# A gated graph step on one Trainium2 core: kept sums added by VectorE instead of merged by TensorE, one early tile more, and pass 2's tiles a step sooner

## The chip, the cores and the metric

The kernel runs on one core of a Trainium2 chip. The metric is the device time of one execution in microseconds (us); lower is better. Before the change it was 345.53 us, the median of 3 runs (345.31 to 345.88). The trace comes from one further, profiled execution.

## What is computed

With 4096 nodes of 64 features and one adjacency matrix `adj` (4096 x 4096, f32, mostly zeros), layer 0 is two gated steps and a layer norm, and layer 1 a sum over each node's last 100 neighbours with weights that halve from one to the next:

```python
def _ggc(x, adj, W, wih, whh, bih, bhh):
    m = adj @ (x @ W)
    gi, gh = m @ wih.T + bih, x @ whh.T + bhh
    r, z = sigmoid(i_r + h_r), sigmoid(i_z + h_z)
    n = tanh(i_n + r * h_n)
    return (1.0 - z) * n + z * x
h = relu(_ggc(x, adj, ...W1)); h = relu(_ggc(h, adj, ...W2))
x = layernorm(x + h)
support = x @ weight
rank = cumsum(adj != 0, axis=1); deg = rank[:, -1:]
k = minimum(deg, 100); pos = rank - (deg - k)
w = (adj != 0) * where(pos > 0, 0.5 ** (k - pos), 0.0)
x = layernorm(x + w @ support + bias)
```

## The kernel before, in words

**Tiling.** The 4096 nodes are 8 chunks of 512 (`NCH`). The matrix comes from memory in pairs of row tiles, 512 KB each: 16 pairs (`NP`) for each chunk. Pairs go into a ring of seven slots (`stream`, `SLOTS`), and a load waits until the pair seven places before it was used by TensorE and read by its mask. SyncE issues the loads in the order of `LOADS`.

**Pass 1** goes through the chunks b = 0 to 7. TensorE multiplies each pair with the first step's input (`product1`, L514) and, where the second step's input for it exists already (`TRI`), also with that. Those partial sums of the second product are set aside for chunks 0 to 4 (`KEPT`): ScalarE copies one half from PSUM into `kept` (chunk 0: `m_high`) at L754, and VectorE adds the other half (`keep_add`, L1109). Between its pairs TensorE runs the recurrence of the chunk before: `gates` (L569), `node` (L598) and a count of the neighbours. VectorE makes a 0/1 mask of each pair (`mask`, L1049); for the pairs in `BY_SIGN` ScalarE does it with a Sign and a Square (`sign_mask`, L757). VectorE also adds up masks and begins the codes.

**Codes and tiles.** The running neighbour count passes from row tile to row tile. `chain` (L1085) is one tile: a subtraction of the mask from the running count (L1096), and the code made of both (L1101). 32 tiles follow each other. The first `N_EARLY` (15) are done in three parts of the columns (`PARTS`: chunks 0 to 2, 3 to 5, 6 and 7), the first two parts in pass 1 at the steps of `CHAIN_EARLY`, the third in pass 2; the others are done whole. After the tile (3, 0) the count is clamped from below over all columns (L1106, "the maximum"). `CHAIN` says which tiles VectorE does in which stage of pass 2, and `CHAIN_CUT` how many of them stand ahead of the sum of squares (L1207), how many between it and `make_x1s` (L1209, the instruction "x1s" L1214), and the rest stands behind.

**Pass 2** has the steps g = 8 to 15 of the recurrence (the second gated step, chunks in descending order). In stage t (t = 1 to 8, g = 7 + t):

- TensorE (`chunk2`, L716): gates(g), two shares of layer 1 (`share`, L618), four pairs of the next chunk, node(g), two shares, the remaining pairs. From stage 7 on there are no pairs, only shares with gates and nodes between them. A chunk whose partial sum was kept gets it back on TensorE: in `product2`, after its first pair, two matmuls of the kept sum with an identity add it in PSUM (L556).
- ScalarE (L907 to 919): two sigmoids (L779), tanh (L786), `high` (the upper half of chunk g+1's product copied to `m_high`, L745), `state` (L802), then expansions (`expand`, L833: a block's codes into bf16 weights for the share, instruction L842), square (L822) of the new nodes, expansions, `split_high` (L826, instruction L832) once x1s is there, expansions. The three numbers in `ACT_EXPANDS[t]` are the expansions in these three places.
- VectorE (L1264 to 1285): first step of the gate's n (L1128), the new state (to L1144), the residual (L1150), `combine` (L1119, the sum of the lower half and `m_high`), tiles, sum of squares, tiles, x1s, tiles, each with expansions by `DVE_EXPANDS[t]` (L1241).
- GpSimd: reciprocal roots (L968), the low half of the support (L982), the bias added (L977).

A share waits for its expansion and for the low half of its support. Each expansion has a place to write to (`PLACE`: weight buffers, dead parts of the codes, `kept` as "k", a dead part of `hx` as "h"). `BY_DVE` and `BY_ACT` say who expands which block, in what order. After stage 8 come the last shares, the last sums and the output (`ACT_END`, `DVE_END`).

Of the kernel before, what the change touches and what calls it, by code (L numbers as in the profile page):

```python
# [50 lines left out]
KEPT = range(0, 5)  # L51
M2_BANK = {0: 3, 1: 1, 2: 2, 3: 3, 4: 2, 5: 3, 6: 1, 7: 2}
# [44 lines left out]
    for first, then in ((1, 2), (1, 2), (2, 4), (3, 5), (3, 5), (4, 6), (5, 8), (6, 9))]  # L97
# [6 lines left out]
CHAIN_EARLY = ({3: (11, 13, 15), 4: (4, 7, 10, 13), 5: (3, 5, 7, 9, 11, 13, 15), 6: (4,)},  # L104
               {6: (10, 11, 12, 13, 14, 14), 7: (2, 3, 5, 6, 7, 8, 9, 10, 12)})
N_EARLY = sum(len(steps) for steps in CHAIN_EARLY[0].values())

BY_SIGN = {5: (8, 11, 13), 6: (8, 9, 11, 13, 14), 7: (1, 8, 9, 11, 13, 14)}
# [42 lines left out]
     if block not in BY_DVE] + \  # L151
    [(4, 3), REST[0], REST[1]] + \
    [block for block in REST[2:] if block not in BY_DVE]
ACT_EXPANDS = {1: (0, 2, 1), 2: (1, 2, 2), 3: (1, 3, 2), 4: (1, 2, 2), 5: (1, 2, 2),
               6: (1, 2, 2), 7: (0, 1, 1), 8: (0, 2, 4)}
DVE_EXPANDS = {1: (0, 0, 0), 2: (0, 0, 0), 3: (0, 0, 0), 4: (0, 0, 1), 5: (0, 0, 1), 6: (0, 0, 3),
# [18 lines left out]
PLACE_USED.update({"m": len(LOADS), "x": NCH * NP, "k": USED[2 * NCH - 3] + 2})  # L175
# [46 lines left out]
CHAIN = [chain_tiles(*x) for x in ((0, 6), (6, 12), (12, 16), (16, 21), (21, 25), (25, 29), (29, 32),  # L222
# [4 lines left out]
def build(nc, adj_t, x_pairs, w1, consts, consts2, bias, out):  # L227
    with ExitStack() as ctx:
# [261 lines left out]
        def _(pe):  # L490
# [46 lines left out]
            def product2(s, q):  # L537
# [202 lines left out]
        def _(act):  # L740
# [93 lines left out]
            def expand(j, i):  # L834
# [72 lines left out]
            for t in range(1, NCH + 1):  # L907
# [90 lines left out]
        def _(dve):  # L998
# [265 lines left out]
            for t in range(1, NCH + 1):  # L1264
# [4 lines left out]
                if t < NCH:  # L1269
                    combine(g + 1)  # L1270
# [107 lines left out]
```

## Time and profile before

| | us |
|---|---|
| median of the runs shown (3) | 345.53 |
| the profiled execution, its own time | 346.18 |
| span of its trace, first to last instruction | 344.1 |
| TensorE busy (matmul) | 328.7 |
| VectorE busy | 299.2 |
| ScalarE busy | 187.6 |
| GpSimd busy | 47.2 |
| moved by DMA | 107.85 MB, of it 106.37 MB read |

The profile is one execution. Its own time is 2.1 us above the span, for what lies before the first and after the last instruction. Busy matmul time is modelled and overlaps at its ends, so a row that starts before the row ahead of it has ended is no error. TensorE's granted clock is at full rate (2.4 GHz) for all of the work. Times in the rows count from the start of the span. Pass 1 ends at about 192 us, pass 2's pairs at about 294 us.

### The profile page before, as it was taken

What the parts mean: (1) busy time and instruction counts of PE and PEld (TensorE: products, weight loads), DVE (VectorE), ACT (ScalarE), POOL (GpSimd) and SP (SyncE); (2) the same over time, 40 slices, a digit from 0 to 9 for tenths busy, and PEclk for the clock granted to TensorE, in tenths of its full rate; (3) what the DMA queues carried; (4) which work ended last, traced back from release to release, by engine and by line L of the source; (5) the groups of instructions that cost most, each with busy time, mean ns of one, the idle gap of its engine ahead of it and who ended that gap; (6) DMA issues with size and microseconds to landing.
All of it is one profiled execution on the core that took longest, in us unless ns stands there. A gap on an engine that the chain in (4) does not pass through costs nothing.

```text
span 344.1 us, 6780 instructions
## 1 busy us (share of the span) xinstructions
PE 328.7 (96%) x2540; PEld 154.0 (45%) x2540; DVE 299.2 (87%) x494; ACT 187.6 (55%) x245; POOL 47.2 (14%) x50
## 2 busy tenths in 40 slices
PE   1998999999999999999999999999999999999993
PEld 0442334333333333333333333546364544789993
DVE  0689879899999999997999678878999999968996
ACT  0203304105122047068467437897977869768995
POOL 2000000000000000000000001250514232233275
PEclk9999999999999999999999999999999999999999
DMA  6999999999999998999898999998999996000003
GB/s 240 414 410 409 410 407 410 404 402 367 399 396 370 366 392 327 351 360 352 291 336 301 378 368 381 392 344 324 339 379 391 346 381 249 4 16 4 2 2 123
DMA packets 32143, 107.85 MB, mean 313 GB/s; under 512 B 3568, under 2 KB 6512, under 8 KB 32112
## 3 DMA queue, kind: packets, MB, share of 16 engines
q1 hardware_dynamic: 31248, 106.15, 81.4%
q10 hardware_dynamic: 864, 1.28, 1.1%
q8 instruction: 20, 0.33, 0.4%
q14 instruction: 11, 0.09, 0.1%
HBM read 106.37 MB, written 1.05 MB: 312 GB/s over the span
## 4 chain that ended last, share of the span: by engine, by line
PE 78%; DMA 10%; DVE 8%; issue 2%; POOL 0%; ACT 0%; POOLq 0%; ACTq 0%; DVEq 0%; SPq 0%
PE m_acc L509 41%; PE out L509 17%; DMA stream<-in_adj_t 9%; PE out L647 8%; PE gate_ps L585 4%; DVE codes L1241 3%; PE gate_ps L592 3%; PE m_acc L647 2%; DMA w<-in_w 2%; PE gate_ps L609 1%; PE gate_ps L614 1%; DVE s_in L1298 1%; DVE codes L1052 1%; DVE stream L1305 1%; PE m_acc L556 1%
## 5 line engine op out<-in xcount | busy, mean ns | idle before, releaser
L509 PE MATMUL m_acc<-stream,s_in 128*64 128x512 f32 x488 | 119.1, 596 | 1.2 <-DMA stream<-in_adj_t 0.9
L1052 DVE TENSOR_SCALAR codes<-stream 128x1024 uint8<-128x1024 f32 x109 | 71.8, 686 | 6.4 <-DMA stream<-in_adj_t 6.2
L509 PE MATMUL out<-stream,s_mid 128*64 128x512 f32 x264 | 66.3, 593 | 0.0
L968 POOL TENSOR_TENSOR rstd<-stat,mhalf 128x4 f32<-128x4 f32 (+1 forms) x17 | 25.6, 1510 | 277.2 <-DVE stat L1207 277.1
L509 PEld LDWEIGHTS m_acc<-stream,s_in 128*64 128x64 f32 x488 | 32.8, 136 | 63.7 <-issue 48.4
L509 PE MATMUL m_acc<-stream,s_mid 128*64 128x512 f32 x224 | 51.8, 600 | 0.2 <-DMA stream<-in_adj_t 0.2
L1101 DVE SCALAR_TENSOR_TENSOR codes<-codes,run 128x384 uint32<-128x384 uint32 (+2 forms) x62 | 45.4, 732 | 2.1
L1096 DVE TENSOR_TENSOR run<-run,codes 128x768 uint16<-128x768 uint16 (+2 forms) x61 | 43.6, 715 | 2.0
L745 ACT ACTIVATE m_high<-m_acc 64x512 f32<-64x512 f32 x13 | 7.7, 594 | 56.3 <-PE m_acc L509 47.7
L842 ACT ACTIVATE wexp<-codes,code_bias 128x2048 uint16<-128x2048 uint8 x18 | 35.7, 1992 | 0.1
L509 PEld LDWEIGHTS out<-stream,s_mid 128*64 128x64 f32 x264 | 18.9, 137 | 37.1 <-issue 36.4
L779 ACT ACTIVATE rz<-gate_ps,b_rz 128x256 f32<-128x256 f32 x32 | 13.4, 468 | 37.7 <-PE gate_ps L592 37.6
L509 PEld LDWEIGHTS m_acc<-stream,s_mid 128*64 128x64 f32 x224 | 14.6, 136 | 26.4 <-issue 25.3
L842 ACT ACTIVATE codes<-codes,code_bias 128x2048 uint16<-128x2048 uint8 x12 | 23.6, 1990 | 0.0
L1069 DVE TENSOR_TENSOR wexp<-wexp,codes 128x2048 uint16<-128x2048 uint16 x16 | 19.6, 1225 | 2.5 <-issue 2.0
L1241 DVE TENSOR_SCALAR codes<-codes 128x2048 uint16<-128x2048 uint8 x15 | 18.7, 1285 | 0.0
L786 ACT ACTIVATE n_g<-t_n,const 128x256 f32<-128x256 f32 x16 | 8.1, 508 | 15.0 <-DVE t_n L1132 14.8
L764 ACT ACTIVATE codes<-codes 128x1024 uint8<-128x1024 int8 x14 | 14.8, 1057 | 0.4
L761 ACT ACTIVATE codes<-stream 128x1024 int8<-128x1024 f32 x13 | 13.6, 1044 | 0.2 <-DMA stream<-in_adj_t 0.2
L802 ACT ACTIVATE mx<-hx 64x256 f32<-64x256 f32 x32 | 13.2, 414 | 0.8
L1128 DVE SCALAR_TENSOR_TENSOR t_n<-gate_ps,const,rz 128x256 f32<-128x256 f32 x16 | 7.7, 479 | 6.6 <-ACT rz L779 6.6
L1002 DVE COPY s_in<-gate_ps 128x256 f32<-128x256 f32 x8 | 3.4, 419 | 11.1 <-PE gate_ps L500 11.1
(179 smaller groups left out, 413.4 us busy)
## 6 DMA issues: line engine op xcount, KB each, us to landing
stream<-in_adj_t SPq DMA_DIRECT2D x192, 512.0 KB, 6.1
wexp<-in_adj_t SPq DMA_DIRECT2D x2, 512.0 KB, 5.5
late<-in_adj_t SPq DMA_DIRECT2D x2, 512.0 KB, 6.6
third<-in_x_pairs SPq DMA_DIRECT2D x8, 128.0 KB, 6.2
out_nodes<-stream SPq DMA_DIRECT2D x7, 128.0 KB, 2.0
hx<-in_x_pairs ACTq DMA_DIRECT2D x1, 512.0 KB, 7.1
third<-in_adj_t SPq DMA_DIRECT2D x1, 512.0 KB, 8.0
run<-in_adj_t SPq DMA_DIRECT2D x1, 512.0 KB, 9.5
```

Of the source, the lines that this page charges most:

```text
L509: last = nc.tensor.matmul(to[D * u:D * (u + 1), :], state[:, t * D:(t + 1) * D], data[:, u * CW:(u + 1) * CW], start=start[u], stop=stop)
L585: nc.tensor.matmul(to[e * D:(e + 1) * D, 0:HW], w_rz[layer][:, part * D:(part + 1) * D], mx[:, e * HW:(e + 1) * HW], start=True, stop=True)
L647: last = nc.tensor.matmul(end_bank(i, t)[:, t * P:(t + 1) * P], w[:, k * CW + t * P:k * CW + (t + 1) * P], half[:, k, :, :], start=first a ...
L761: nc.scalar.activation(to.bitcast(I8), loaded(n), ACT.Sign)\
L764: nc.scalar.activation(to, to.bitcast(I8), ACT.Square).then_inc(squares_made, 1)
L842: nc.scalar.activation(weights(j, i).bitcast(U16), block(j, i), ACT.Relu, bias=code_bias[:, :], scale=float(P)).then_inc(by_act, 1)
L968: nc.gpsimd.tensor_tensor(rstd[:, r, nodes], stat[:, r, nodes], mhalf[:, nodes], ALU.pow).then_inc(rstd_made, 1)
L1052: nc.vector.tensor_scalar(edges(p // 2, b, 2 * (p % 2), 2), loaded(n), 0.0, None, ALU.not_equal).then_inc(mask_made, 1)
L1069: nc.vector.tensor_tensor(to, left, right, ALU.add).then_inc(sum_made, 1)
L1096: nc.vector.tensor_tensor(running(n + 1, U16)[:, to], running(n, U16)[:, to], tile_edges(c, k, U16)[:, to], ALU.subtract)\
L1101: nc.vector.scalar_tensor_tensor(at, at, EDGE_BIT, running(n, U32)[:, to], ALU.logical_shift_left, ALU.bitwise_or)\
L1241: nc.vector.tensor_scalar(weights(j, i).bitcast(U16), block(j, i), float(P), -float(P * CODE_ZERO), ALU.mult, ALU.add)\
```

## The change

- TensorE no longer merges the kept sums (the matmuls at L556 go). For the steps 11 to 15 (`WITH_KEPT`) VectorE makes `m_high` by one addition of the upper half in PSUM and the kept sum (`high_kept`), between residual and combine of the stage before the step, and ScalarE's `high` goes for those steps.
- 16 tiles instead of 15 are begun in pass 1. In chunk 4 there are six early tiles instead of four, in chunk 6 none of part 0 (before: one, at step 4) and seven of part 1 (before: six).
- Chunk 4 gets three ScalarE masks, at its steps 8, 11 and 13.
- Stage 2 of pass 2 does the tiles 12 to 17 (before 12 to 15), stage 3 18 to 21 (16 to 20), stage 4 22 to 25 (21 to 24), stage 5 26 to 28 (25 to 28).
- Three expansions move from VectorE (one each from stages 4, 5 and 6) to ScalarE (one more each in stages 4, 5 and 7).
- Block (4, 1) is expanded into "h"; "k" is free after step 14's `m_high`.

```diff
--- before.py
+++ after.py
@@ -49,6 +49,7 @@
 KEPT = range(0, 5)
+WITH_KEPT = range(NCH + 3, 2 * NCH)
 M2_BANK = {0: 3, 1: 1, 2: 2, 3: 3, 4: 2, 5: 3, 6: 1, 7: 2}
 M2_AFTER = {3: 0, 4: 2, 5: 3, 6: 1, 7: 4}
@@ -101,11 +102,11 @@
 PARTS = (slice(0, 3), slice(3, 6), slice(6, NCH))
 GUARD_IN = {3: 0, 6: 1}
-CHAIN_EARLY = ({3: (11, 13, 15), 4: (4, 7, 10, 13), 5: (3, 5, 7, 9, 11, 13, 15), 6: (4,)},
-               {6: (10, 11, 12, 13, 14, 14), 7: (2, 3, 5, 6, 7, 8, 9, 10, 12)})
+CHAIN_EARLY = ({3: (11, 13, 15), 4: (3, 5, 7, 10, 13, 15), 5: (3, 5, 7, 9, 11, 13, 15)},
+               {6: (10, 11, 12, 13, 14, 14, 15), 7: (2, 3, 5, 6, 7, 8, 9, 10, 12)})
 N_EARLY = sum(len(steps) for steps in CHAIN_EARLY[0].values())
-BY_SIGN = {5: (8, 11, 13), 6: (8, 9, 11, 13, 14), 7: (1, 8, 9, 11, 13, 14)}
+BY_SIGN = {4: (8, 11, 13), 5: (8, 11, 13), 6: (8, 9, 11, 13, 14), 7: (1, 8, 9, 11, 13, 14)}
@@ -137,9 +138,10 @@
 PLACE = {block: ("w0", "w1", "x" if n < 4 * ALONG else "k")[n % 3]
          for n, block in enumerate(ORDER[:RING])}
+PLACE[4, 1] = "h"
 PLACE.update({block: f"d{n}" for n, block in zip((1, 3, 2, 5, 4, 7, 6, 9, 8), AHEAD)})
 PLACE.update({block: (PLACES + AGAIN + AGAIN)[n] for n, block in enumerate(REST)})
-BY_DVE = [AHEAD[4], AHEAD[6], AHEAD[7], AHEAD[8]] + \
+BY_DVE = [AHEAD[7]] + \
     [REST[n] for n in (2, 5, 7, 9, 11)] + \
     [(6, 5), (7, 3), (7, 4), (7, 5), (0, 6), (3, 6), (5, 6), (6, 6), (7, 6), (1, 7), (2, 7), (5, 7)]
@@ -149,11 +151,11 @@
     [block for j in range(1, 4) for block in
      [(j, 3), (j + 1, 0), (j + 1, 1), AHEAD[2 * j - 1], (j + 1, 2), AHEAD[2 * j]]
      if block not in BY_DVE] + \
-    [(4, 3), REST[0], REST[1]] + \
-    [block for block in REST[2:] if block not in BY_DVE]
-ACT_EXPANDS = {1: (0, 2, 1), 2: (1, 2, 2), 3: (1, 3, 2), 4: (1, 2, 2), 5: (1, 2, 2),
-               6: (1, 2, 2), 7: (0, 1, 1), 8: (0, 2, 4)}
-DVE_EXPANDS = {1: (0, 0, 0), 2: (0, 0, 0), 3: (0, 0, 0), 4: (0, 0, 1), 5: (0, 0, 1), 6: (0, 0, 3),
+    [(4, 3), REST[0], REST[1], (5, 3), (6, 0), AHEAD[8]] + \
+    [block for block in REST[2:] if block not in BY_DVE + [(5, 3), (6, 0)]]
+ACT_EXPANDS = {1: (0, 2, 1), 2: (1, 2, 2), 3: (1, 3, 2), 4: (1, 3, 2), 5: (1, 3, 2),
+               6: (1, 2, 2), 7: (0, 2, 1), 8: (0, 2, 4)}
+DVE_EXPANDS = {1: (0, 0, 0), 2: (0, 0, 0), 3: (0, 0, 0), 4: (0, 0, 0), 5: (0, 0, 0), 6: (0, 0, 2),
                7: (1, 0, 1), 8: (1, 1, 5)}
 ACT_END = (1, 1, 2, 1, 1, 0, 0, 0)
 DVE_END = (1, 1, 3, 1, 1, 0, 0)
@@ -172,7 +174,7 @@
 PLACE_USED = {f"s{i}": 1 + max(n for n in range(len(LOADS)) if n % SLOTS == i)
               for i in range(SLOTS)}
-PLACE_USED.update({"m": len(LOADS), "x": NCH * NP, "k": USED[2 * NCH - 3] + 2})
+PLACE_USED.update({"m": len(LOADS), "x": NCH * NP})
 AT_RZ, AT_N, AT_W2 = 0, P, P + D
 AT_BI, AT_BH, AT_BNI, AT_BNH = P + 2 * D, P + 2 * D + 4, P + 2 * D + 8, P + 2 * D + 10
@@ -219,7 +221,7 @@
-CHAIN = [chain_tiles(*x) for x in ((0, 6), (6, 12), (12, 16), (16, 21), (21, 25), (25, 29), (29, 32),
+CHAIN = [chain_tiles(*x) for x in ((0, 6), (6, 12), (12, 18), (18, 22), (22, 26), (26, 29), (29, 32),
                                    (32, 32), (32, 32))]
 CHAIN_CUT = [(1, 2), (1, 3), (2, 3), (2, 3)] + [(1, 2)] * 3 + [(0, 1)] * 2
@@ -548,13 +550,6 @@
                     pe.wait_ge(m_ready, {3: NCH, 4: NCH - 1}.get(s, s + 7))
                 pair_in(pe, n)
                 pair(n, q, s_mid, acc_bank(g), [first] * 2, n == USED[g] - 1).then_inc(pair_used, 1)
-                if first and ch in KEPT:
-                    half, _, part = kept_part(ch)
-                    pe.wait_ge(m2_kept, len(KEPT))
-                    for u in range(2):
-                        nodes = slice(u * HW, (u + 1) * HW)
-                        nc.tensor.matmul(acc_bank(g)[u * D:(u + 1) * D, nodes], ident2[half, :],
-                                         part[:, nodes], start=False, stop=False)
             def count(b):
                 pe.wait_ge(s_bf_made, b + 1)
@@ -839,6 +834,8 @@
                     act.wait_ge(pair_used, PLACE_USED[PLACE[j, i]])
                 if PLACE[j, i] == "h":
                     act.wait_ge(h_made, NCH + 4)
+                if PLACE[j, i] == "k":
+                    act.wait_ge(high_copied, 2 * NCH - 1)
                 nc.scalar.activation(weights(j, i).bitcast(U16), block(j, i), ACT.Relu,
                                      bias=code_bias[:, :], scale=float(P)).then_inc(by_act, 1)
@@ -910,7 +907,8 @@
                 sigmoids(g)
                 tanh(g)
                 if t < NCH:
-                    high(g + 1)
+                    if g + 1 not in WITH_KEPT:
+                        high(g + 1)
                     state(g + 1)
                 expand_next(before_square)
                 square(t - 1)
@@ -1101,7 +1099,7 @@
                 nc.vector.scalar_tensor_tensor(at, at, EDGE_BIT, running(n, U32)[:, to],
                                                ALU.logical_shift_left, ALU.bitwise_or)\
                     .then_inc(codes_made, 1)
-                if (j, k) == (3, 0):
+                if (j, k) == (3, 0) and part == 2:
                     dve.wait_ge(codes_made, i)
                     nc.vector.tensor_scalar(run[(n + 2) % 2][:, :], run[(n + 1) % 2][:, :],
                                             float(GUARD), None, ALU.max).then_inc(run_made, 1)
@@ -1118,6 +1116,14 @@
                     dve.wait_ge(gates_done, g)
                 nc.vector.tensor_tensor(mx[0:D, :], acc_bank(g)[0:D, :], m_high[0:D, :], ALU.add)\
                     .then_inc(m_ready, 1)
+
+            def high_kept(g):
+                _, _, part = kept_part(2 * NCH - 1 - g)
+                dve.wait_ge(pair_used, USED[g])
+                dve.wait_ge(m2_kept, len(KEPT))
+                dve.wait_ge(m_ready, g)
+                nc.vector.tensor_tensor(m_high[0:D, :], acc_bank(g)[D:P, :], part, ALU.add)\
+                    .then_inc(high_copied, 1)
             def n_input(g):
                 layer = g // NCH
@@ -1238,6 +1244,8 @@
                     dve.wait_ge(pair_used, PLACE_USED[PLACE[j, i]])
                 if PLACE[j, i] == "h":
                     dve.wait_ge(h_made, NCH + 4)
+                if PLACE[j, i] == "k":
+                    dve.wait_ge(high_copied, 2 * NCH - 1)
                 nc.vector.tensor_scalar(weights(j, i).bitcast(U16), block(j, i), float(P),
                                         -float(P * CODE_ZERO), ALU.mult, ALU.add)\
                     .then_inc(by_dve, 1)
@@ -1266,6 +1274,8 @@
                 n_input(g)
                 new_h(g)
                 residual(g)
+                if g + 1 in WITH_KEPT:
+                    high_kept(g + 1)
                 if t < NCH:
                     combine(g + 1)
                 first, second = CHAIN_CUT[t]
```

## Rows read from the trace of the kernel before

**Rows 1.** Page, part 1: busy us, share of the span, instructions, of each engine

```profile
PE 328.7 (96%) x2540; PEld 154.0 (45%) x2540; DVE 299.2 (87%) x494; ACT 187.6 (55%) x245; POOL 47.2 (14%) x50
```

**Rows 2.** Chain of waits, 205 to 250 us: start, length, what

```profile
207.83 6.70 DMA stream<-in_adj_t
...
226.23 0.58 PE m_acc L556 x4
```

**Rows 3.** Timeline of VectorE: start, length, engine, line, op, tiles, form, count, [idle]

```profile
204.76 0.41 DVE L1096 TENSOR_TENSOR run<-run,codes 128x512 uint16<-128x512 uint16 x1
...
205.73 0.42 DVE L1096 TENSOR_TENSOR run<-run,codes 128x512 uint16<-128x512 uint16 x1
...
226.06 1.22 DVE L1096 TENSOR_TENSOR run<-run,codes 128x2048 uint16<-128x2048 uint16 x1
...
228.58 2.65 DVE L1106 TENSOR_SCALAR run<-run 128x4096 uint8<-128x4096 uint8 x1
233.28 0.48 DVE L1128 SCALAR_TENSOR_TENSOR t_n<-gate_ps,const,rz 128x256 f32<-128x256 f32 x1 [2.06 <-ACT rz L779]
...
235.71 0.43 DVE L1150 SCALAR_TENSOR_TENSOR third<-t_n,third 128x256 f32<-128x256 f32 x1
...
244.35 0.68 DVE L1214 TENSOR_TENSOR late<-gate_ps,rstd 128x512 f32<-128x512 f32 x1
...
246.20 1.58 DVE L1101 SCALAR_TENSOR_TENSOR codes<-codes,run 128x1024 uint32<-128x1024 uint32 x1
...
250.63 0.47 DVE L1128 SCALAR_TENSOR_TENSOR t_n<-gate_ps,const,rz 128x256 f32<-128x256 f32 x1
...
265.38 1.22 DVE L1241 TENSOR_SCALAR codes<-codes 128x2048 uint16<-128x2048 uint8 x1
266.52 0.47 DVE L1128 SCALAR_TENSOR_TENSOR t_n<-gate_ps,const,rz 128x256 f32<-128x256 f32 x1
```

**Rows 4.** Timeline of ScalarE in pass 2, same columns

```profile
232.77 0.84 ACT L779 ACTIVATE rz<-gate_ps,b_rz 128x256 f32<-128x256 f32 x2 [1.15 <-PE gate_ps L592]
234.25 0.51 ACT L786 ACTIVATE n_g<-t_n,const 128x256 f32<-128x256 f32 x1 [0.64 <-DVE t_n L1132]
...
236.28 2.00 ACT L842 ACTIVATE wexp<-codes,code_bias 128x2048 uint16<-128x2048 uint8 x1
...
245.06 0.42 ACT L832 ACTIVATE codes<-late 128x256 f16<-128x256 f32 x1
...
249.17 0.81 ACT L779 ACTIVATE rz<-gate_ps,b_rz 128x256 f32<-128x256 f32 x2
...
300.96 0.38 ACT L822 ACTIVATE sq<-gate_ps 128x256 f32<-128x256 f32 x1 [0.96 <-PE gate_ps L609]
...
306.27 0.84 ACT L779 ACTIVATE rz<-gate_ps,b_rz 128x256 f32<-128x256 f32 x2 [0.17 <-PE gate_ps L592]
```

**Rows 5.** Groups of instructions: form, count | busy us, mean ns | idle before

```profile
L764 ACT ACTIVATE codes<-codes 128x1024 uint8<-128x1024 int8 x14 | 14.8, 1057 | 0.4
...
L745 ACT ACTIVATE m_high<-m_acc 64x512 f32<-64x512 f32 x13 | 7.7, 594 | 56.3 <-PE m_acc L509 47.7 <-PE out L509 8.4
...
L1112 DVE TENSOR_TENSOR kept<-kept,out 64x512 f32<-64x512 f32 x4 | 2.7, 683 | 0.5 <-ACT kept L754 0.4
```

**Rows 6.** Groups of instructions on VectorE, shapes kept apart

```profile
L1052 DVE TENSOR_SCALAR codes<-stream 128x1024 uint8<-128x1024 f32 x109 | 71.8, 686 | 6.4 <-DMA stream<-in_adj_t 6.2
...
L1101 DVE SCALAR_TENSOR_TENSOR codes<-codes,run 128x384 uint32<-128x384 uint32 x30 | 16.7, 558 | 1.0
L1096 DVE TENSOR_TENSOR run<-run,codes 128x768 uint16<-128x768 uint16 x30 | 16.6, 552 | 0.7
```

**Rows 7.** Timeline of ScalarE, chunk 4 of pass 1

```profile
117.23 0.59 ACT L745 ACTIVATE m_high<-m_acc 64x512 f32<-64x512 f32 x1 [7.59 <-PE m_acc L509]
```

**Rows 8.** Timeline of GpSimd, stage 2

```profile
229.04 2.77 POOL L977 TENSOR_TENSOR s_in<-late,third 128x256 f32<-128x256 f32 x1
```

**Rows 9.** Timeline of TensorE: node(11)

```profile
254.47 0.72 PE L609 MATMUL gate_ps<-to_x1s,third 64*128 64x128 f32 x8
```

## The prediction

> **What bounds the kernel now.** I read the page first: TensorE is busy for 96% of the span, VectorE for 87% [rows 1]. So work taken from TensorE is worth something only where TensorE, and nobody it waits for, sets the pace. I write "stage t" for the part of pass 2 between gates(7+t) and gates(8+t), g10 for step 10 of the recurrence, and so on. The chain of waits through pass 2 is TensorE work end to end, with one break: at the end of stage 1 it goes back through a load issued at 207.83 that took 6.70 to land [rows 2]. The timelines of the other engines then show who is nearly late. In stage 2 VectorE ends with a full tile and the maximum and then idles 2.06 us before the first step of g10 at 233.28 [rows 3]. In stage 3 it does not idle at all: g11's first step is at 250.63, although ScalarE had begun its sigmoids at 249.17 [rows 3, 4]. ScalarE is as tight there: its high half follows VectorE's x1s (244.35, 0.68 long) at 245.06, and two expansions later, with no idle, come the sigmoids [rows 3, 4]. So stage 3 has three engines in step, and a microsecond added on VectorE before x1s reaches the sigmoids whole.
>
> **TensorE's part.** Each merge of a kept sum holds TensorE 0.58 us [rows 2]; there are five, one in each of stages 1 to 5, so 2.9 us leave its queue. The first is worth nothing: it runs at about 212, and the pair after next waits for the load that lands at 207.83 + 6.70 = 214.53, whose issue hangs on an earlier pair. What can be gained is 4 x 0.58 = 2.3 us.
>
> **VectorE's kept add.** Its nearest row is the kept add of pass 1, 64x512 with one operand in PSUM, 683 ns; with the semaphore before the sum that waits for it I take 0.72 us. It stands in stages 3 to 7 between the residual and the sum, in front of that stage's tiles and x1s. ScalarE's copy of the high half (594 ns, a slot of 0.6) goes from the same stages [rows 5]. The Trainium skill ("VectorE: DVE Perf Modes", Specifications) says that VectorE sits closer to SBUF and ScalarE closer to PSUM, which speaks against moving a PSUM read to VectorE; the rows agree, 683 against 594 ns, and the sum has that price already.
>
> **Pass 1.** Chunk 4 gets two more early tiles of three blocks, 552 + 558 ns each [rows 6], 1.1 to 1.2 us with the semaphore, and loses three masks of 0.69 us [rows 6]: VectorE is longer by about 0.2 us. ScalarE's three pairs of Sign and Square cost it six times about 1.06, 6.3 us [rows 5], where it idles up to 7.59 us at a time [rows 7]. Chunk 6 loses one early tile (step 4) and gets one (step 15), ahead of the sum for gates(6). Loads in chunk 4 are issued later by up to 1.1 us at steps 3 to 7, and I take the cost as nothing because of the ring of seven slots; if that cover is gone, TensorE waits. A small gain, half a mask (0.3 us), is not excluded where ScalarE's masks free slots sooner; a loss could reach the part of 1.1 us that the ring does not cover, say half. I bound pass 1 between -0.3 and +0.5 us, and take 0.
>
> **Stage 2 of pass 2, where the step sooner is paid.** Behind x1s stood one full tile and the maximum. Now there stand: one small tile (start to start 205.73 - 204.76 = 0.97), the maximum (2.65), and two full tiles (228.58 - 226.06 = 2.52 each) [rows 3]. From 226.06 that is 0.97 + 2.69 + 5.04, so g10's first step can start at 234.7. GpSimd's add of the bias is there too: next to the maximum it took 2.77 us and ended 0.58 after it [rows 8], and beside full tiles of stage 3 it stretched a VectorE instruction to 1.58, from 1.22 [rows 3]. Bounds: nothing, or two such stretches, 0.7 us. I take one, 0.35, since most of the bias add will again lie under the maximum. So g10's first step is at 235.1 instead of 233.28: +1.8 us. Of the 3.4 us added, 2.06 were covered by the idle time, but TensorE's saving had wanted that idle time.
>
> The Trainium skill ("SBUF — State Buffer", Who interferes with whom) has it that VectorE and GpSimd share a port pair under a lock, and that the second to start blocks fully. By that rule the bias add, once it holds the pair, would cost VectorE up to its whole unobstructed length and the sum would come to +1.4 us; the row shows a stretch of 0.35, and I go by the row.
>
> **Stage 3.** From g10's first step to x1s was 244.35 - 233.28 = 11.07 [rows 3], now 0.72 more: x1s at 246.9, done at 247.6. ScalarE has by then done its expansions (free at 235.1 + 0.97 + 1.41 + 1.9 + 0.4 + 5.7 = 245.5, the pieces as in the next part) and waits. From its high half to the next sigmoids are 249.17 - 245.06 = 4.11 [rows 4]: g11's sigmoids at 251.7, +2.5 us. The tile fewer behind x1s helps nobody, since VectorE then waits for ScalarE. TensorE stalls at node(11): it could be there at 254.47 - 1.2 = 253.3 [rows 9], but the state comes at 251.7 + 0.5 + 2.85 = 255.05 (2.85 is from g10's first step to the end of the residual: 235.71 + 0.42 - 233.28 [rows 3]).
>
> **Stages 4 to 6.** ScalarE's round without a wait is 1.48 (sigmoids to tanh), 1.41 (tanh to the first expansion, 236.28 - 234.25 less the copy's 0.6 to 0.62), 1.9 (one expansion), 0.4 (square), 5.7 (three), 4.11 (high half and two) [rows 4] = 15.0 us, with the expansion that VectorE hands over. Stage 4: sigmoids of g12 at 266.7. VectorE's round was 266.52 - 250.63 = 15.89; less its expansion (1.14), plus 0.72, it is 15.5 [rows 3], so g12's first step is at 252.2 + 15.5 = 267.7. Stage 5: tanh 0.97 later, then 1.41 + 1.9 + 0.4 + 5.7 + 4.11: sigmoids of g13 at 282.2. Stage 6 has one expansion fewer and x1s ends the wait: 282.7 + (11.07 - 2.57 + 0.72) + 0.68 = 292.6, and 4.11 more: 296.7. By then the lateness has shrunk to 0.9 us, since these rounds are shorter than TensorE's stages of before.
>
> **Stage 7.** Here ScalarE gets one expansion more, and nothing hides it: state of g14 at 296.7 + 3.35, square of the new nodes at 300.9 (before 300.96 [rows 4]; 0.1 and 0.76 lie between state, node and square), then 0.4, two expansions 3.8, high half 0.33, one expansion 1.9: g15's sigmoids at 307.3. Before, they were at 306.27 [rows 4]. That is +1.1 us. Behind g15 both kernels do the same work in the same order (seven VectorE expansions, six of ScalarE in stage 8, the same at the end), so the end moves rigidly.
>
> **The sum.** +1.1 us on the profiled execution (346.18 us, span 344.1). The median of the runs shown, 345.53, is 0.65 lower; with the same step the forecast is 346.6 us. From no change this measurement can tell about 0.2%, 0.7 us.
>
> **The rivals.**
> 1. *The early tiles are hidden* (faster). If VectorE reached g10 by 232.7, ScalarE's rounds of 15.0 would start 2.4 us sooner and stay ahead of TensorE's gates. TensorE would keep its 2.3 us as far as g14; in stage 7 ScalarE's round, 0.5 + 2.85 + 0.1 to the node, 0.76 to the square and 6.4 more, is 10.6 from sigmoids to sigmoids, which costs 0.1: -2.2 us, 343.3. It decides at one place: VectorE's arrival at g10. The 2.06 us idle speaks for it, the 3.4 us of added work against it. If the lateness there is under half, the time crosses that of before. Chance 0.20.
> 2. *A wash.* No stretch by GpSimd (-0.35 at g10) and rounds 0.1 us shorter than I read them bring the sum to between -0.7 and +0.7: 345.5. The rounds of ScalarE catch up 0.3 to 1.7 us a stage, and a small error there repeats four times. Chance 0.24.
> 3. *The forecast*: lateness of stage 3 carried to g15 by ScalarE, +0.7 to +1.5. Chance 0.44.
> 4. *Pass 1 pays too*: the later load issues of chunk 4 and the tile at step 15 of chunk 6 reach TensorE (0.5 us), and both full tiles are stretched (0.35): +2.0, 347.5. The 0.2 us that VectorE gains in work is small, and chunk 5 already runs with the same ScalarE masks, which speaks against it. Chance 0.12.
>
> The range goes from nearly the whole gain of rival 1 to the sum of rival 4, and leaves out the ends of both: 343.4 to 347.5. Faster 0.20, same 0.24, slower 0.56.
>
> **What would show it.** Right: no TensorE time on the merge; VectorE without idle between stage 2 and g10's first step near 235; ScalarE waiting 2 us for x1s in stage 3; TensorE idle at node(11); g15's sigmoids near 307.3. TensorE's idle time in pass 2 should grow by more than the 2.9 us that it lost in work. Wrong: g10's first step before 233.3, or no TensorE wait at the nodes, or a DMA wait in chunk 4 that the kernel before lacks.

## The result and the profile after

The changed kernel takes **346.96 us**, the median of 5 runs (346.41 to 347.13), against 345.53: a ratio of 1.0033, 95% interval 1.002 to 1.0047. It is slower by 1.4 us, or 0.3%. The forecast was 346.6. The profiled execution took 346.65, its span 344.9 (before 346.18 and 344.1), so in the two traces only 0.8 us of difference is to be found: the profiled execution of before lay 0.65 above its median, this one 0.31 below.

The page's first part, as [rows 1]:

```profile
PE 325.1 (94%) x2520; PEld 153.9 (45%) x2520; DVE 298.3 (86%) x497; ACT 195.2 (57%) x249; POOL 46.5 (13%) x50
```

TensorE's busy time is 3.6 us less, and the kernel is still longer. Where the difference went shows in the windows from the start of gates(8) to the start of node(15), in the kernel before and then in the changed one (columns: the window, its length, busy us and instructions of TensorE, of its weight loads, of VectorE, ScalarE, GpSimd, then granted clock, DMA share, GB/s):

```profile
205.15:309.81 104.66, 104.45 (x974) 55.94 (x971) 93.68 (x133) 85.20 (x90) 29.67 (x21) 1.00 0.79 296
```
```profile
205.12:310.57 105.45, 101.51 (x954) 55.53 (x950) 92.36 (x135) 86.75 (x88) 28.91 (x21) 1.00 0.79 295
```

TensorE's busy time in the stretch fell by 2.94 us, the five merges, and its idle time rose from 0.21 to 3.94, by 3.73. The difference is the stretch's 0.79 us more, and that is the whole difference of the two spans. Ahead of it nothing moved: in pass 1 the last pair of chunk 7 starts at 190.70 (before 190.74). Behind node(15) nothing moved either: the spans differ by the same 0.8.

The timeline of VectorE in stages 2 and 3, as [rows 3] (start, length, engine, line, operation, tiles, form, count, [idle before and what ended it]):

```profile
226.56 2.29 DVE L1104 TENSOR_SCALAR run<-run 128x4096 uint8<-128x4096 uint8 x1
228.89 1.58 DVE L1094 TENSOR_TENSOR run<-run,codes 128x2048 uint16<-128x2048 uint16 x1
230.50 1.64 DVE L1099 SCALAR_TENSOR_TENSOR codes<-codes,run 128x1024 uint32<-128x1024 uint32 x1
232.24 1.23 DVE L1094 TENSOR_TENSOR run<-run,codes 128x2048 uint16<-128x2048 uint16 x1
233.50 1.23 DVE L1099 SCALAR_TENSOR_TENSOR codes<-codes,run 128x1024 uint32<-128x1024 uint32 x1
234.64 0.47 DVE L1134 SCALAR_TENSOR_TENSOR t_n<-gate_ps,const,rz 128x256 f32<-128x256 f32 x1
...
237.06 0.42 DVE L1156 SCALAR_TENSOR_TENSOR third<-t_n,third 128x256 f32<-128x256 f32 x1
237.52 0.69 DVE L1125 TENSOR_TENSOR m_high<-m_acc,kept 64x512 f32<-64x512 f32 x1
238.31 0.68 DVE L1117 TENSOR_TENSOR mx<-m_acc,m_high 64x512 f32<-64x512 f32 x1
...
246.61 0.68 DVE L1220 TENSOR_TENSOR late<-gate_ps,rstd 128x512 f32<-128x512 f32 x1
...
251.92 0.48 DVE L1134 SCALAR_TENSOR_TENSOR t_n<-gate_ps,const,rz 128x256 f32<-128x256 f32 x1 [1.88 <-ACT rz L774]
```

Behind the maximum stand two full tiles, and g10's first step comes without idle at 234.64 (before 233.28, after 2.06 us of idle). From there the lateness passes to ScalarE, as [rows 4]:

```profile
231.55 0.84 ACT L774 ACTIVATE rz<-gate_ps,b_rz 128x256 f32<-128x256 f32 x2 [0.34 <-PE gate_ps L587]
235.61 0.51 ACT L781 ACTIVATE n_g<-t_n,const 128x256 f32<-128x256 f32 x1 [3.22 <-DVE t_n L1138]
...
247.32 0.42 ACT L827 ACTIVATE codes<-late 128x256 f16<-128x256 f32 x1 [2.36 <-DVE late L1220]
...
251.43 0.81 ACT L774 ACTIVATE rz<-gate_ps,b_rz 128x256 f32<-128x256 f32 x2
...
266.25 0.82 ACT L774 ACTIVATE rz<-gate_ps,b_rz 128x256 f32<-128x256 f32 x2
...
281.90 0.81 ACT L774 ACTIVATE rz<-gate_ps,b_rz 128x256 f32<-128x256 f32 x2
...
296.60 0.82 ACT L774 ACTIVATE rz<-gate_ps,b_rz 128x256 f32<-128x256 f32 x2
...
307.18 0.81 ACT L774 ACTIVATE rz<-gate_ps,b_rz 128x256 f32<-128x256 f32 x2
```

The sigmoids of g10 are on time at 231.55, but tanh waits 3.22 us for VectorE and the high half 2.36 us for x1s. ScalarE then begins g11's sigmoids 2.3 us later than before, g12's 0.8, g13's 0.9, g14's 0.8 and g15's 0.9. TensorE then has waits that the kernel before lacks. Its timeline, as [rows 9]:

```profile
237.54 0.72 PE L604 MATMUL gate_ps<-to_x1s,third 64*128 64x128 f32 x8 [0.58 <-DVE third L1156]
...
247.43 1.08 PE L580 MATMUL gate_ps<-mx,third 128*64 128x256 f32 x8 [1.06 <-DVE late L1220]
...
254.83 0.71 PE L604 MATMUL gate_ps<-to_x1s,third 64*128 64x128 f32 x8 [0.24 <-DVE third L1156]
...
300.00 0.72 PE L604 MATMUL gate_ps<-to_x1s,third 64*128 64x128 f32 x8 [0.70 <-DVE third L1156]
...
304.88 1.08 PE L580 MATMUL gate_ps<-mx,third 128*64 128x256 f32 x8 [0.48 <-DVE late L1220]
...
310.57 0.72 PE L604 MATMUL gate_ps<-to_x1s,third 64*128 64x128 f32 x8 [0.34 <-DVE third L1156]
```

### The profile page after: what moved, and what is told of

Its sections match the earlier page's. It is cut to its first block and busy times, and to the rows that moved or that the text cites. A ratio compares the mean times of both kernels' runs of the same rounds, so it can differ in the third digit from the quotient of the medians.

```text
span 344.9 us, 6749 instructions
## 1 busy us (share of the span) xinstructions
PE 325.1 (94%) x2520; PEld 153.9 (45%) x2520; DVE 298.3 (86%) x497; ACT 195.2 (57%) x249; POOL 46.5 (13%) x50
## 5 line engine op out<-in xcount | busy, mean ns | idle before, releaser
L1050 DVE TENSOR_SCALAR codes<-stream 128x1024 uint8<-128x1024 f32 x106 | 70.1, 685 | 6.5 <-DMA stream<-in_adj_t 6.4
L511 PE MATMUL m_acc<-stream,s_mid 128*64 128x512 f32 x224 | 50.5, 597 | 0.0
L1099 DVE SCALAR_TENSOR_TENSOR codes<-codes,run 128x384 uint32<-128x384 uint32 (+2 forms) x64 | 46.1, 720 | 2.2
L740 ACT ACTIVATE m_high<-m_acc 64x512 f32<-64x512 f32 x8 | 4.8, 595 | 52.2 <-PE m_acc L511 43.4
L839 ACT ACTIVATE codes<-codes,code_bias 128x2048 uint16<-128x2048 uint8 x15 | 29.6, 1989 | 0.0
L759 ACT ACTIVATE codes<-codes 128x1024 uint8<-128x1024 int8 x17 | 18.0, 1057 | 0.5
L756 ACT ACTIVATE codes<-stream 128x1024 int8<-128x1024 f32 x16 | 16.7, 1043 | 0.0
L1249 DVE TENSOR_SCALAR codes<-codes 128x2048 uint16<-128x2048 uint8 x12 | 14.6, 1256 | 0.0
```

The costliest lines, as they stand in the source:

```text
L511: last = nc.tensor.matmul(to[D * u:D * (u + 1), :], state[:, t * D:(t + 1) * D], data[:, u * CW:(u + 1) * CW], start=start[u], stop=stop)
L756: nc.scalar.activation(to.bitcast(I8), loaded(n), ACT.Sign)\
L759: nc.scalar.activation(to, to.bitcast(I8), ACT.Square).then_inc(squares_made, 1)
L1050: nc.vector.tensor_scalar(edges(p // 2, b, 2 * (p % 2), 2), loaded(n), 0.0, None, ALU.not_equal).then_inc(mask_made, 1)
L1099: nc.vector.scalar_tensor_tensor(at, at, EDGE_BIT, running(n, U32)[:, to], ALU.logical_shift_left, ALU.bitwise_or)\
L1249: nc.vector.tensor_scalar(weights(j, i).bitcast(U16), block(j, i), float(P), -float(P * CODE_ZERO), ALU.mult, ALU.add)\
```

## The experiments

**The theory:** TensorE's saving is real, but the two tiles' work in stage 2 exceeds VectorE's room there, and ScalarE's rounds carry the lateness to g15. The rivals: VectorE's kept adds by themselves are the loss; pass 1 is; or ScalarE's extra expansion in stage 7. Ratios are against the kernel before, run on the same chip (its medians there: 345.52 to 345.64); each has its 95% interval. Unless said otherwise the diff is against the changed kernel.

**1. tiles_back.** Only the tiles of pass 2 go back to their stages.

```diff
-CHAIN = [chain_tiles(*x) for x in ((0, 6), (6, 12), (12, 18), (18, 22), (22, 26), (26, 29), (29, 32),
+CHAIN = [chain_tiles(*x) for x in ((0, 6), (6, 12), (12, 16), (16, 21), (21, 25), (25, 29), (29, 32),
```

> The changed kernel, but pass 2's tiles in the stages of before (12 to 15, 16 to 20, 21 to 24, 25 to 28, 29 to 31). Theory A (the tiles of stage 2 make VectorE late at g10, ScalarE carries it on): g10's first step comes right after its sigmoids, near 232.1 instead of 234.64, TensorE does not wait at gates(11), VectorE sets the pace in stages 3 to 5 (g13's first step near 281.1 instead of 282.39), g15's sigmoids near 305.7 instead of 307.18: 1.5 us less than the changed kernel, about 345.4 us. Theory B (the kept adds on VectorE are the whole cost): no change, 347.0.

Measured: 346.02 us, ratio 1.0017 (1.0008 to 1.0026); 0.9 us below the changed kernel. In stage 2 VectorE now idles. The first steps of g10, g11 and g12 on its timeline:

```profile
232.08 0.48 DVE L1134 SCALAR_TENSOR_TENSOR t_n<-gate_ps,const,rz 128x256 f32<-128x256 f32 x1 [3.21 <-ACT rz L774]
...
250.32 0.48 DVE L1134 SCALAR_TENSOR_TENSOR t_n<-gate_ps,const,rz 128x256 f32<-128x256 f32 x1
...
265.97 0.48 DVE L1134 SCALAR_TENSOR_TENSOR t_n<-gate_ps,const,rz 128x256 f32<-128x256 f32 x1
```

g10 is 2.6 us sooner than in the changed kernel, but stage 3 has its fifth tile again and a kept add on top, so g11's first step follows its tiles without idle at 250.32 though its sigmoids began at 248.88. Against experiment 5, which has one tile fewer in stage 3, g11's first step is 1.4 us late, and g12's and g13's are late by the same 1.4: the lateness that the change makes in stage 2 is made in stage 3 instead. The time lies between the theory's number and the rival's, 0.6 us above the first: VectorE's rounds of 15.65 us (265.97 - 250.32) are 0.2 longer than I had priced, which is the kept add's slot (see below).

**2. stage7_later.** The expansion that stage 7 got goes to stage 8.

```diff
-               6: (1, 2, 2), 7: (0, 2, 1), 8: (0, 2, 4)}
+               6: (1, 2, 2), 7: (0, 2, 0), 8: (0, 2, 5)}
```

> The changed kernel, but ScalarE's last expansion of stage 7 moved behind stage 8's (0,2,0 and 0,2,5). Theory A: g15's sigmoids wait no more for ScalarE but for gates(15), which itself waits for x1s: 306.6 instead of 307.18, 0.6 us less, 346.4. Rival: ScalarE's total work bounds the end, no change (347.0), or a share waits for its weights and it is slower.

Measured: 347.54 us, 1.0059 (1.0047 to 1.0072). **A miss**, and slower than the changed kernel by 0.6. g15's sigmoids came at 306.60, 0.6 sooner, so the step in stage 7 is as I read it; but ScalarE has no room in stage 8 either. Its squares for the last sums come at 324.74 (changed kernel 323.28), and VectorE waits for one:

```profile
325.17 0.42 DVE L1213 TENSOR_REDUCE stat<-stream 128x4 f32<-128x260 f32 x1 [1.19 <-ACT stream L921]
```

The same instruction starts at 324.33 in the changed kernel, without a wait. My claim that the end moves rigidly with g15's sigmoids holds for the change itself, which leaves stage 8 alone, and not for one that puts work into stage 8.

**3. kept_adds_only.** The kernel before with the kept sums moved to VectorE and nothing else; the diff is against the kernel before, and holds the change's hunks on `PLACE`, `PLACE_USED`, `expand` and `high_kept` besides:

```diff
+WITH_KEPT = range(NCH + 3, 2 * NCH)
...
-                if first and ch in KEPT:
...
-                    high(g + 1)
+                    if g + 1 not in WITH_KEPT:
+                        high(g + 1)
...
+                if g + 1 in WITH_KEPT:
+                    high_kept(g + 1)
```

> The kernel before with the kept adds on VectorE alone (merge off TensorE, high half off ScalarE for the steps 11 to 15, block (4, 1) in the other place), masks, early tiles, tile stages and expansions as before. Theory A: VectorE has no slack in stages 3 to 6, so 0.72 us a stage add up there: g13's first step near 283.4 (before 282.40), g14's near 298.7 (before 297.03), 2 us slower than before, 347.5. Theory D (TensorE bounds, its 2.9 us come off): 343.3.

Measured: 348.96 us, 1.01 (1.0086 to 1.0113), 3.3 us above the kernel before. The sign is as expected, the size 1.5 us over. VectorE's first steps of g11, g12 and g13 stand at 249.91, 266.70 and 283.49: rounds of 16.79 us against 15.89 before, so one kept add costs **0.90 us** in its place. TensorE waits longer from node to node, from node(11) to node(13):

```profile
252.81 0.71 PE L604 MATMUL gate_ps<-to_x1s,third 64*128 64x128 f32 x8 [0.63 <-DVE third L1156]
...
269.61 0.72 PE L604 MATMUL gate_ps<-to_x1s,third 64*128 64x128 f32 x8 [1.03 <-DVE third L1156]
...
286.40 0.71 PE L604 MATMUL gate_ps<-to_x1s,third 64*128 64x128 f32 x8 [1.88 <-DVE third L1156]
```

So the kept adds do need VectorE relieved elsewhere; the other parts of the change buy back about 2 of these 3.3 us.

**4. pass1_only.** The kernel before with the change's part in pass 1; the diff is against the kernel before.

```diff
-CHAIN_EARLY = ({3: (11, 13, 15), 4: (4, 7, 10, 13), 5: (3, 5, 7, 9, 11, 13, 15), 6: (4,)},
-               {6: (10, 11, 12, 13, 14, 14), 7: (2, 3, 5, 6, 7, 8, 9, 10, 12)})
+CHAIN_EARLY = ({3: (11, 13, 15), 4: (3, 5, 7, 10, 13, 15), 5: (3, 5, 7, 9, 11, 13, 15)},
+               {6: (10, 11, 12, 13, 14, 14, 15), 7: (2, 3, 5, 6, 7, 8, 9, 10, 12)})
...
-BY_SIGN = {5: (8, 11, 13), 6: (8, 9, 11, 13, 14), 7: (1, 8, 9, 11, 13, 14)}
+BY_SIGN = {4: (8, 11, 13), 5: (8, 11, 13), 6: (8, 9, 11, 13, 14), 7: (1, 8, 9, 11, 13, 14)}
...
-                if (j, k) == (3, 0):
+                if (j, k) == (3, 0) and part == 2:
```

> The kernel before with the early tiles and the three ScalarE masks of the change alone. Theory A: pass 1 ends at the same time, the smaller tile 15 only lengthens VectorE's idle time before g10 (2.06 to about 3.7 us): 345.5, no change. Rival C (pass 1 pays for it): slower by 0.3 us or more, with a TensorE wait for a load in chunk 4 or at gates(6).

Measured: 345.70 us, 1.0009 (0.9995 to 1.0023): no change that can be told. Pass 1 is not where the loss is.

**5. one_tile_sooner.** The changed kernel, but the tiles one instead of two sooner in stage 2.

```diff
-CHAIN = [chain_tiles(*x) for x in ((0, 6), (6, 12), (12, 18), (18, 22), (22, 26), (26, 29), (29, 32),
+CHAIN = [chain_tiles(*x) for x in ((0, 6), (6, 12), (12, 17), (17, 21), (21, 25), (25, 29), (29, 32),
```

> The changed kernel with one tile sooner in place of two: stage 2 does the tiles 12 to 16, stage 3 17 to 20, stages 4 and 5 four each. Theory A (the loss is VectorE's arrival at g10): stage 2's VectorE work ends at about 232.1, just when g10's sigmoids are there, x1s of stage 3 near 243.9, g13's first step near 280.1, g15's sigmoids near 304.7 (before 306.27, changed kernel 307.18): 344.3 us, faster than both kernels. Theory B (kept adds on VectorE are the loss wherever the tiles stand): as with the tiles back, 346.0, or slower.

Measured: **344.53 us, 0.997 (0.9958 to 0.9982)**, faster than both: 2.4 us below the changed kernel and 1.1 below the one before (0.3%). VectorE in stage 2 and at g11:

```profile
226.16 2.29 DVE L1104 TENSOR_SCALAR run<-run 128x4096 uint8<-128x4096 uint8 x1
228.49 1.58 DVE L1094 TENSOR_TENSOR run<-run,codes 128x2048 uint16<-128x2048 uint16 x1
230.09 1.64 DVE L1099 SCALAR_TENSOR_TENSOR codes<-codes,run 128x1024 uint32<-128x1024 uint32 x1
231.66 0.48 DVE L1134 SCALAR_TENSOR_TENSOR t_n<-gate_ps,const,rz 128x256 f32<-128x256 f32 x1
...
248.95 0.48 DVE L1134 SCALAR_TENSOR_TENSOR t_n<-gate_ps,const,rz 128x256 f32<-128x256 f32 x1 [1.89 <-ACT rz L774]
```

The last tile of stage 2 ends as the sigmoids of g10 (231.15) hand over; VectorE loses nothing, and stage 3 has four tiles with its kept add. g15's sigmoids come at 305.05, 2.1 sooner than in the changed kernel. This is the theory's own place, and one full tile there decides between faster and slower.

**6. merge_back.** The changed kernel with the merges on TensorE again.

```diff
-WITH_KEPT = range(NCH + 3, 2 * NCH)
+WITH_KEPT = range(0)
...
+                if first and ch in KEPT:
+                    half, _, part = kept_part(ch)
+                    pe.wait_ge(m2_kept, len(KEPT))
+                    for u in range(2):
+                        nodes = slice(u * HW, (u + 1) * HW)
+                        nc.tensor.matmul(acc_bank(g)[u * D:(u + 1) * D, nodes], ident2[half, :],
+                                         part[:, nodes], start=False, stop=False)
```

> The changed kernel with the kept sums merged by TensorE again (and the high halves copied by ScalarE), all else as changed. Theory A: g10's first step stays at 234.6, x1s of stage 3 comes 0.72 us sooner (245.9), g15's sigmoids near 306.5 instead of 307.18, so 0.7 us less, 346.3: the merge that was taken off TensorE was worth nothing here. Theory D (TensorE's 2.9 us are what the change gains, and other parts lose more): 2 us or more slower than the changed kernel.

Measured: 347.31 us, 1.0052 (1.0036 to 1.0068). **A miss by 1.0.** Steps 10 and 11 come sooner as expected (first steps 234.37 and 250.75), but TensorE now has 2.9 us more and is the one that comes late from g14 on (gates(14) at 293.95 against 293.10). ScalarE there, and with TensorE's late node its wait at the square:

```profile
295.64 0.84 ACT L781 ACTIVATE rz<-gate_ps,b_rz 128x256 f32<-128x256 f32 x2 [0.22 <-PE gate_ps L594]
...
300.84 0.38 ACT L824 ACTIVATE sq<-gate_ps 128x256 f32<-128x256 f32 x1 [1.71 <-PE gate_ps L611]
...
307.25 0.81 ACT L781 ACTIVATE rz<-gate_ps,b_rz 128x256 f32<-128x256 f32 x2
```

g15's sigmoids are back at the changed kernel's 307.18. I had let ScalarE alone carry the time from g11 on. The intervals of this kernel and the changed one overlap: with the lateness of stage 2 in place, what the 2.9 us taken from TensorE are worth, less what the kept adds cost VectorE, is 0.35 us by the medians and cannot be told from nothing.

**7. before_one_sooner.** The kernel of experiment 4, and against it the tiles one sooner: merges and expansions as in the kernel before.

```diff
-CHAIN = [chain_tiles(*x) for x in ((0, 6), (6, 12), (12, 16), (16, 21), (21, 25), (25, 29), (29, 32),
+CHAIN = [chain_tiles(*x) for x in ((0, 6), (6, 12), (12, 17), (17, 21), (21, 25), (25, 29), (29, 32),
```

> The kernel before with the pass 1 part of the change (16 early tiles, three ScalarE masks) and one tile sooner (12 to 16, 17 to 20), kept sums merged by TensorE, expansions as before. Theory A: VectorE's idle time of 3.7 us before g10 takes the tile (2.5 us), g11's first step moves from 250.04 to about 249.4, then TensorE's own pace bounds (its merges are back): 345.2, 0.3 to 0.6 us less than before. If it reaches 344.3 too, the kept adds have no part in the gain of one_tile_sooner.

Measured: 345.60 us, 0.9997 (0.9985 to 1.0009). No change, and the small gain of 0.3 to 0.6 us that was expected is not there either: VectorE still idles 0.73 us before g10's first step, and sooner helpers gain nothing while TensorE has its merges. The gain of experiment 5 therefore needs the rest of the change: with the kept adds on VectorE and the expansions on ScalarE it is 344.53, without them 345.60. These two went together; no run separates them beside one early tile.

**8. expansions_back.** The changed kernel with the three expansions on VectorE again.

```diff
-BY_DVE = [AHEAD[7]] + \
+BY_DVE = [AHEAD[4], AHEAD[6], AHEAD[7], AHEAD[8]] + \
...
-ACT_EXPANDS = {1: (0, 2, 1), 2: (1, 2, 2), 3: (1, 3, 2), 4: (1, 3, 2), 5: (1, 3, 2),
-               6: (1, 2, 2), 7: (0, 2, 1), 8: (0, 2, 4)}
-DVE_EXPANDS = {1: (0, 0, 0), 2: (0, 0, 0), 3: (0, 0, 0), 4: (0, 0, 0), 5: (0, 0, 0), 6: (0, 0, 2),
+ACT_EXPANDS = {1: (0, 2, 1), 2: (1, 2, 2), 3: (1, 3, 2), 4: (1, 2, 2), 5: (1, 2, 2),
+               6: (1, 2, 2), 7: (0, 1, 1), 8: (0, 2, 4)}
+DVE_EXPANDS = {1: (0, 0, 0), 2: (0, 0, 0), 3: (0, 0, 0), 4: (0, 0, 1), 5: (0, 0, 1), 6: (0, 0, 3),
```

> The changed kernel with the three expansions given back to VectorE (stages 4, 5, 6) and ScalarE's counts as before. Theory A (VectorE is the fuller engine, the hand-over was needed by the kept adds): g13's first step near 283.0 instead of 282.39, g14's near 298.3 instead of 297.09, g15's sigmoids near 308.3 instead of 307.18: 1.1 us more, 348.0. Rival E (the longer ScalarE rounds and the extra expansion of stage 7 are what made it slower): 1 to 2 us less, 345.5.

Measured: 347.95 us, 1.0076 (1.0059 to 1.0093), as expected. g12's first step comes at 268.34 (changed kernel 267.58), g15's sigmoids at 308.45: handing these three expansions to ScalarE is worth 1.0 us, in spite of the stage 7 that it lengthens.

**9. two_sooner_only.** The kernel of experiment 4, and against it the changed `CHAIN`: merges and expansions as before.

```diff
-CHAIN = [chain_tiles(*x) for x in ((0, 6), (6, 12), (12, 16), (16, 21), (21, 25), (25, 29), (29, 32),
+CHAIN = [chain_tiles(*x) for x in ((0, 6), (6, 12), (12, 18), (18, 22), (22, 26), (26, 29), (29, 32),
```

> The kernel before with the pass 1 part and the changed tile stages (12 to 17, 18 to 21, 22 to 25, 26 to 28) alone; kept sums merged by TensorE, expansions as before. Theory A as refined (VectorE is late at g10, but it takes ScalarE's longer rounds to carry the lateness to the end): g10's first step near 234.7, g11's sigmoids near 250.9, but stages 4 and 5 have ScalarE rounds of 13.7 us and catch up; g14's and g15's sigmoids at TensorE's pace, 306.2 or less: 345.7, no change against before. Rival F (tiles two steps sooner cost what they cost at g10, whatever follows): 346.9 or more.

Measured: 346.19 us, 1.0019 (1.0008 to 1.003), between the theory's number and the rival's. g10's first step is late here too (234.27), but from g12 on ScalarE, without the third expansions of stages 4 and 5 and the extra one of stage 7, waits for gates (its waits at the sigmoids are 1.21, 0.82 and 0.42 us), and g15's sigmoids start at 306.04. The lateness of stage 2 alone is caught up in the trace (span 343.9 against 344.1). But the traced execution, 345.66 us, is also the fastest of the twelve, and the medians keep 0.7 us of difference; no row shows where, and that stays open.

**10. no_sign_masks.** The changed kernel without the three ScalarE masks of chunk 4.

```diff
-BY_SIGN = {4: (8, 11, 13), 5: (8, 11, 13), 6: (8, 9, 11, 13, 14), 7: (1, 8, 9, 11, 13, 14)}
+BY_SIGN = {5: (8, 11, 13), 6: (8, 9, 11, 13, 14), 7: (1, 8, 9, 11, 13, 14)}
```

> The changed kernel with chunk 4's three masks on VectorE again. Theory A: VectorE has 2.1 us more in chunk 4, loads of chunk 5 are issued as much later, where the changed kernel has only 0.75 us between landing and use: TensorE waits 1.3 us or more for loads in chunk 5, 348.3. Rival G (the ring hides it as it hid the early tiles): 347.0, no change.

Measured: 347.88 us, 1.0066 (1.0048 to 1.0083), 0.9 above the changed kernel and 0.4 below what was expected. The windows of chunk 4, without the masks and then with them (columns as above):

```profile
98.40:121.30 22.90, 22.16 (x119) 7.82 (x116) 22.36 (x39) 5.25 (x11) 0.00 (x0) 1.00 0.92 340
```
```profile
98.40:121.30 22.90, 22.90 (x126) 8.24 (x124) 22.36 (x40) 11.38 (x17) 0.00 (x0) 1.00 0.96 365
```

VectorE is nearly full in both (22.36 of 22.90). Without ScalarE's masks less is loaded in the same time (340 against 365 GB/s), and TensorE waits for a load:

```profile
117.41 1.08 PE L511 MATMUL m_acc<-stream,s_in 128*64 128x512 f32 x4 [0.74 <-DMA stream<-in_adj_t]
```

This wait lies in chunk 4, not in chunk 5, where I had expected it and where TensorE is busy throughout. Two more waits for loads (0.62 and 0.19 us) follow behind node(8). So "pass 1 costs nothing" is true of the early tiles of chunk 4 only together with the masks; without the masks the changed kernel is 0.9 us longer.

## Why the prediction was right, point by point

The steps, forecast and measured, all in us from the start of the span:

| step | before | forecast | after |
|---|---|---|---|
| g10, first step | 233.28 | 235.1 | 234.64 |
| x1s of stage 3 | 244.35 | 246.9 | 246.61 |
| g11, sigmoids | 249.17 | 251.7 | 251.43 |
| g12, sigmoids | 265.49 | 266.7 | 266.25 |
| g13, sigmoids | 281.00 | 282.2 | 281.90 |
| g14, sigmoids | 295.77 | 296.7 | 296.60 |
| g15, sigmoids | 306.27 | 307.3 | 307.18 |

- **The path.** The steps came in the order and at the places that the prediction gives: g10's first step 0.46 us before the forecast, and every later step 0.1 to 0.45 before it. TensorE's idle time in pass 2 grew by 3.7 us, over the 2.9 that I gave as the sign. Experiment 5 confirms where it is decided: one full tile fewer in stage 2 turns the result from +1.4 to -1.1 us against the kernel before. Rival 1's price of -2.2 us was too high: with the tiles of stage 2 hidden the gain is 1.1, in the medians. Its sum let ScalarE's rounds of 15.0 set the later stages, but in experiment 5 VectorE's rounds with four tiles and a kept add do: 15.66 us (g11's first step 248.95, g12's 264.61, g13's 280.27). g14's sigmoids are 1.3 us sooner than before and not 2.3.
- **What the 0.9 us at g15 is made of.** The lateness of 0.8 us at g14's sigmoids does not itself reach the end. The next step, the square in stage 7, hangs on TensorE's node(14), and both come a little sooner than in the kernel before, whose square is at 300.96 [rows 4]. The changed kernel's:

```profile
300.77 0.38 ACT L817 ACTIVATE sq<-gate_ps 128x256 f32<-128x256 f32 x1 [1.32 <-PE gate_ps L604]
```

  From there to g15's sigmoids are 6.41 us, against 5.31 before: the 1.1 us of ScalarE's extra expansion in stage 7, as the prediction's paragraph on stage 7 has it. The lateness of stage 2 has used up what TensorE had gained by node(14), and stage 7 then shows as a loss. Experiment 5 pays the same 6.41, but from a square at 298.64, 2.3 sooner than before, and is left with 1.2 of it at g15.
- **g10's first step: two errors and an early start, partly luck.** I took one stretch of 0.35 us by GpSimd; there were two, of 0.35 and 0.41 (1.58 and 1.64 us instead of 1.23). The maximum was 0.36 shorter than in [rows 3], which cancels one of them, so the work from the small tile to g10's first step took 8.99 us against 9.04 forecast. VectorE also began it 0.42 us sooner. In the kernel before and then in the changed one x1s of stage 2 stands at:

```profile
225.46 0.69 DVE L1214 TENSOR_TENSOR late<-gate_ps,rstd 128x512 f32<-128x512 f32 x1 [0.46 <-POOL rstd L968]
```
```profile
225.04 0.69 DVE L1220 TENSOR_TENSOR late<-gate_ps,rstd 128x512 f32<-128x512 f32 x1 [0.46 <-POOL rstd L966]
```

  The prediction also says that 3.4 us are added in stage 2. By its own terms it is 3.49, and 3.84 with the stretch; its +1.8 us is 3.84 less the 2.06 of idle time.
- **The first merge.** I had it worth nothing, behind a load. In the changed kernel no load holds TensorE there: gates(9) came at 214.42 instead of 215.55, and gates(10) at 229.85 instead of 231.08. Of the 1.1 us at gates(9), 0.54 went in a wait for GpSimd's low half, and node(9) came 0.49 sooner (222.12 against 222.61); the early x1s above follows from it. How much of that is the merge stays open: from gates(8) to this x1s are 19.92 us here, but with the merges on TensorE they are 19.91 in experiment 4, 20.31 in the kernel before and 20.32 in experiment 7. gates(11), which waits for VectorE, is back at its place of before (247.43 against 247.44).
- **Pass 1** took nothing, as I had it. What hides the tiles was not the ring alone, though: experiment 10 shows that the ScalarE masks are needed as well.
- **The kept add was mis-sized.** I took 0.72. The instruction lasts 0.69, but from the residual's start to the sum's is 1.25 us (237.06 to 238.31). Before it was 0.34, from the residual at 235.71 [rows 3] to the sum at 236.05:

```profile
236.05 0.68 DVE L1119 TENSOR_TENSOR mx<-m_acc,m_high 64x512 f32<-64x512 f32 x1
```

  That makes 0.91, as the rounds of experiment 3 have it (0.90). In the change it shows as 0.2 us wherever VectorE sets the pace: from g10's first step to x1s of stage 3 are 11.97 us against 11.79 forecast, and VectorE's round of stage 4 is 15.66 against 15.5. The early start at g10 covered both. In experiment 1, where VectorE sets the rounds, it explains the 0.6 us. In experiment 3, with five adds, it explains about 0.9 of the 1.5 (an estimate, 5 x 0.18 from the rows); the profiled execution of before lies 0.65 above its median, which is about the rest.
- **The place of TensorE's wait.** I named node(11), which waits 0.24 us. The larger one, 1.06 us, is already at gates(11), since the gates wait for x1s as well; I had overlooked that semaphore. For the time it makes no difference, as ScalarE's high half waits for the same x1s.
- **The end.** g15's sigmoids are 0.9 us late in the traces and the medians differ by 1.43. The forecast put the step of the trace, 1.1, on the median, so that 346.6 lies 0.4 under the result although the step itself was forecast 0.2 too large. Profiled executions scatter by as much as the remaining 0.5: in experiments 1 and 5, with the same work ahead of it, g10's sigmoids start at 231.57 and 231.15. I take it for such scatter; no run tells it apart.

## What to carry to other kernels

Before work is moved to an earlier stage, compare it with the idle time that the receiving stage itself has. Here, with the sixteenth early tile done in pass 1, VectorE idled 3.98 us before g10 (experiment 4). One full tile took 3.25 of them with its stretches and left 0.73 (experiment 7); a second does not fit, and this alone stood between 0.3% faster and 0.3% slower. Work taken from the bounding engine pays only where the helpers' rounds are shorter than its stage. Experiments 3, 5 and 7 are the three cases: in 3 TensorE is relieved and VectorE, with the adds on top, is too slow; in 5 TensorE is relieved and the helpers keep up; in 7 the helpers are sooner and TensorE is not relieved. And when work is handed from one engine to another, price the slot, start to start with the semaphores on both sides, and not the instruction.

## What the runs showed of the hardware

VectorE and GpSimd stretch each other, both ways. These are GpSimd's two instructions of stage 2 in the changed kernel, and the second of them in stage 7, where VectorE is idle beside it:

```profile
227.50 1.89 POOL L980 TENSOR_TENSOR late<-late 128x256 f16<-128x256 f32 x1 [2.49 <-ACT late L827]
229.34 1.71 POOL L975 TENSOR_TENSOR s_in<-late,third 128x256 f32<-128x256 f32 x1
...
306.36 0.72 POOL L975 TENSOR_TENSOR s_in<-late,third 128x256 f32<-128x256 f32 x1
```

The low half fell under the maximum and took 1.89 us, where before, at the end of a full tile and the start of the maximum, it took 1.15. The bias add lay beside the full tile at 228.89: it took 1.71 us instead of the 0.72 that it takes alone, and both of the tile's instructions took 1.58 and 1.64 instead of 1.23. In stage 6 two VectorE expansions beside GpSimd took 1.69 and 1.75 us instead of 1.22.

The Trainium skill ("SBUF — State Buffer", Who interferes with whom) describes an exclusive lock under which the second to start blocks fully. Each stretch here, 0.35 to 0.53 us, is less than a whole instruction of GpSimd alone (0.72), but that does not refute the rule: the low half ends at 229.39, so it was still running when the tile's first instruction began at 228.89, and the traces do not tell which of GpSimd's two stretched which of VectorE's. What they do show is the sum. VectorE loses 0.35 + 0.41 = 0.76 us beside GpSimd's pair in stage 2, and 0.36 + 0.35 = 0.71 in stage 3 of the kernel before. The prediction took one stretch of 0.35 and set the page's price aside, and was too low by the other. Its +1.4 us by the page's rule is close to the measured 1.43 by luck, since the shorter maximum and the early x1s made good more than the second stretch cost.
